# Two transformer layers on one core: attention, the middle and the delta rule's scalars in one block of instructions

## What is computed

```python
x = layernorm(x + attention(x))          # 32 query heads, 8 key heads of 8 dims, rope, causal softmax, @ Wo + bo
x = layernorm(x + ffn8(x))               # silu(x @ w_gate * s) * (x @ w_up * s) @ w_down * s, int8 weights, 1024 wide
x = layernorm(x + delta(x))              # 16 heads of 128
x = layernorm(x + ffn_sign(x))           # relu(x @ sign(up)) @ sign(down)

def delta(x):
    q, k, v = (silu(causal_conv4(x @ W)) for W in (Wq, Wk, Wv))
    alpha, beta = sigmoid(x @ Wa + ba), sigmoid(x @ Wb + bb)
    # per head, for t in order: S = alpha_t * S - beta_t * (S k_t - v_t) k_t^T ;  o_t = S q_t
    return (layernorm(o) * sigmoid(x @ Wg)) @ Wo
```

## Time and profile before

| what | value |
|---|---|
| time of the runs, us | 2126.25, 2126.78 (median), 2129.01 |
| the profiled execution: time, span, us | 2118.2, 2116.5 |
| mean granted TensorE clock, share of full speed | 0.951 |
| busy: PE, DVE, ACT, POOL | 1928.3, 1567.2, 1333.5, 743.7 us |
| attention ends, middle's first product | 511.16, 512.13 us |
| middle ends, delta_heads' first DMA | 667.72, 683.53 us |
| first product of delta_heads | 687.05 us |

### The profile page before, as it was taken

One profiled execution on the slowest core, in us unless ns is written; L12 is line 12 of the kernel. 1 busy time (PEld: TensorE's weight loads), 2 busy tenths in 40 slices (PEclk: granted clock), 3 DMA queues, 4 the chain that ended last, 5 costly groups with the idle time before them and its releaser, 6 DMA issues. The chain is left out here.

```text
span 2116.5 us, 68799 instructions
## 1 busy us (share of the span) xinstructions
PE 1928.3 (91%) x29180; PEld 1458.4 (69%) x29180; DVE 1567.2 (74%) x3017; ACT 1333.5 (63%) x2887; POOL 743.7 (35%) x1037
## 2 busy tenths in 40 slices
PE   7589999996885699999999999999999999999767
PEld 4233333333774578888888888888888888888656
DVE  2699999971754578788888877778788788887356
ACT  1248888884431357677766667667666677676443
POOL 2423444451322223333333333333333333332233
PEclk8779999998996799999999999999999999999879
DMA  3301212101000101011011011011011011010011
GB/s 122 89 21 43 53 31 64 46 18 39 1 1 9 62 12 55 23 42 48 23 49 41 23 44 45 23 37 53 23 35 55 23 40 50 23 34 26 1 43 41
DMA packets 74336, 79.86 MB, mean 38 GB/s; under 512 B 13424, under 2 KB 60912, under 8 KB 74032
## 3 DMA queue, kind: packets, MB, share of 16 engines
q1 hardware_dynamic: 74032, 75.46, 12.3%
HBM read 66.13 MB, written 8.91 MB: 35 GB/s over the span
## 5 line engine op out<-in xcount | busy, mean ns | idle before, releaser
L1711 DVE SCALAR_TENSOR_TENSOR d_acc<-ps,d_par,d_acc 128x1023 f32<-128x1023 f32 (+2 forms) x288 | 365.1, 1268 | 29.5 <-ACT d_acc L1590 28.5
L1403 PE MATMUL ps<-x1p,d_wh 128*128 128x512 f32 x1024 | 358.5, 432 | 16.6 <-DVE d_acc L1711 9.8
L514 ACT ACTIVATE a_prob<-ps 128x512 f32<-128x512 f32 (+2 forms) x640 | 311.3, 560 | 87.3 <-PE ps L483 83.1
L537 DVE TENSOR_REDUCE a_mx<-ps 128x2 f32<-128x1024 f32 (+2 forms) x320 | 336.6, 1111 | 33.5 <-PE ps L467 20.3
L1337 POOL TENSOR_TENSOR d_og_l<-d_o_g,d_og_h 128x512 fp32r<-128x512 f32 x64 | 82.0, 1281 | 426.0 <-ACT d_og_h L1687 426.0
L1403 PE MATMUL ps<-x1p,d_wl 128*128 128x512 f32 x512 | 204.4, 399 | 0.0
L1403 PEld LDWEIGHTS ps<-x1p,d_wh 128*128 128x128 f32 x1024 | 170.8, 194 | 40.1 <-DVE d_acc L1711 10.6
L1590 ACT ACTIVATE d_acc<-ps,d_par 128x512 f32<-128x512 f32 x192 | 149.0, 776 | 72.3 <-PE ps L1403 71.3
L462 PE MATMUL ps<-k,q 48*128 48x512 bf16 (+3 forms) x768 | 142.6, 348 | 34.5 <-DMA k<-scratch_k 20.3
L483 PE MATMUL ps<-q,k 51*128 51x512 bf16 (+2 forms) x640 | 161.4, 364 | 5.6 <-ACT a_prob L514 3.1
L497 PE MATMUL ps<-a_prob,a_v 128*32 128x512 f32 (+3 forms) x1536 | 164.4, 501 | 0.2
(11 more groups left out here) (244 smaller groups left out, 4793.8 us busy)
## 6 DMA issues: line engine op xcount, KB each, us to landing
d_abc<-scratch_alpha SPq DMA_DIRECT2D x32, 512.0 KB, 5.1
d_gb<-scratch_g SPq DMA_DIRECT2D x32, 512.0 KB, 4.0
d_wr<-in_dw SPq DMA_DIRECT2D x16, 512.0 KB, 4.9
scratch_q<-p_parts SPq DMA_DIRECT2D x24, 128.0 KB, 2.4
q<-scratch_q SPq DMA_DIRECT2D x32, 96.0 KB
scratch_y<-a_oT SPq DMA_DIRECT2D x64, 36.0 KB
x_tok<-in_x SPq DMA_DIRECT2D x2, 1024.0 KB
q<-scratch_q SPq DMA_DIRECT2D x32, 64.0 KB
```

The source lines that it names most:

```text
L514: inc(nc.scalar.activation(prob[:, y % PB, g:g + heads, off:], ps[:, PLACE["st", n, x], 0:heads * w].rearrange("p (h c) -> p h c", c=w), A ...
L537: inc(nc.vector.tensor_reduce(out, ps[:, bank:bank + 2, 0:heads * w].rearrange("p r (h c) -> p r h c", c=w), AX.X, ALU.max, negate=True), ...
L1403: last = nc.tensor.matmul(ps[:, bank, :], wp[g][:, k, i, :], x(part), start=(k == 0 and j == 0), stop=(k == KE - 1 and j == 2))
L1711: inc(nc.vector.scalar_tensor_tensor(acc[i][:, d:T], taps[:, 0:T - d], par[p][:, 4 * i + j:4 * i + j + 1], acc[i][:, d:T], ALU.mult, ALU.a ...
```

## The change

The three stages attention, middle and delta_scalars become one block: each function returns its five engine programs, and `one_after_another` writes them behind each other, engine by engine, with semaphores where the barriers were. The phase ends behind delta_scalars.

- **The block around the stages.** Two barriers go. TensorE waits at the end of attention for the last unit's copies out of PSUM. DMAs of the middle (wab, bab, head 0's weights) are issued in load_and_project, behind its own loads. x's transposed copy there takes yT's memory.

```diff
-            load_and_project(nc, ps, x_tok, cst, scratch,
+        load_and_project(nc, ps, x_tok, yT, cst, scratch,
...
+                          "cos": a["c_cos"], "sin": a["c_sin"]}, (w0, ow, hw))
+        with phase(nc) as joint:
+            heads, *rest = attention(nc, layer, ps, x_tok, yT, cst, scratch, ow, w0)
...
+            layers, zs = middle(nc, joint, memory, ps, x_tok, yT, xp, z, cst, ow, w0, hw, *rest)
+            memory.close()
+            one_after_another(nc, joint, heads, layers, delta_scalars(nc, joint, ps, z, sc, cst, alpha_rows, g_rows, zs))
```

```diff
-            E_.walk("POOL", {"v": values, "hide": hide, "cut": cut, "scale": scale})
+        E_.walk("POOL", {"v": values, "hide": hide, "cut": cut, "scale": lambda n: scale(pool, n) if n < UNITS - 1 else None})
...
+        W("nmT", UNITS - 1, 1)
+        W("exp", UNITS - 1, NST)
+        W("o_out", UNITS - 1, 2)
...
+        E_.walk("DVE", {"s1": maxima, "nm": both, "turn": turn, "rec": lambda n: reciprocal(dve, n) if n < UNITS - 1 else None})
+        dve.wait_ge(w.arrived, w.count)
+        for u in range(w.n_up):
+            nc.vector.tensor_copy(w.wu[:, u], w.up[:, u]).then_inc(w.cast, 1)
-            E_.walk("DVE", {"s1": maxima, "nm": both, "turn": turn, "rec": reciprocal})
+    return Programs(sync, gpsimd, tensor, scalar, vector), scaled, reciprocal, scale
...
     self.w, self.n_up = w, w["up"].shape[0]
-        self.arrived, self.count = ctx.enter_context(nc.semaphore("g_w_in")), 16 * (self.n_up + 3)
+        self.arrived, self.count = ctx.enter_context(nc.semaphore("g_w_in")), 16 * (self.n_up + 5)
...
+        self.wu, self.cast = sb("wu", [P, self.n_up, KE, FF], F32R), ctx.enter_context(nc.semaphore("g_cast"))
+        self.wab, self.bab = sb("wab", [P, KE, 2 * H]), sb("bab", [P, 2 * H])
```

```diff
-    with phase(nc) as ctx:
...
-        O_BANK = (6, 4, 2, 6)
+    O_BANK = (6, 4, 6, 6)
+    PROJECT = {1: 2, 5: 3}
...
-        @block.sync
-        def _(sp):
-            sp.dma_start(wab[:], a["wab"].rearrange("(k p) n -> p k n", p=P)).then_inc(ab_in, 16)
-            sp.dma_start(bab[:], a["bab"].partition_broadcast(P)).then_inc(ab_in, 16)
-            hw.fetch(sp, 0)
...
-                if n == 3:
-                    pe.wait_ge(o_freed, 1)
+            pe.wait_ge(scaled, 2 if n < 2 else 4)
+            if n >= 2:
+                pe.wait_ge(o_freed, 2 * n - 3)
...
-                    pe.wait_ge(ab_in, 32)
-                    pe.wait_ge(h_ready, NC * BLK)
+                pe.wait_ge(h_ready, NC * BLK - 1)
...
+        def down_last(c0, c1):
+            if c0 == 0:
+                pe.wait_ge(freed, BLK - 1)
+            for c in range(c0, c1):
+                pe.wait_ge(h_low[c % 2], NC // 2 * (BLK - 1) + c // 2 + 1)
+                for t in range(BT):
+                    for i in range(2):
+                        last = nc.tensor.matmul(ps[:, DOWN + t // 2, (t % 2) * E:(t % 2 + 1) * E], hp[:, 1, i, c, t * P:(t + 1) * P], wd[:, c, :],
+                                                start=(c == 0 and i == 0 and t % 2 == 0), stop=(c == NC - 1 and i == 1), skip_group_check=True)
+            if c1 == NC:
+                last.then_inc(downed, 1)
...
-                    pe.wait_ge(o_freed, 3)
+            if m == 1:
+                pe.wait_ge(o_freed, 2)
...
-            for n in range(3):
+        for n in range(2):
             project(n)
                 up(n, c)
-                    if n == 0 and c == 1:
-                        project(3)
+                if n == 0 and c in PROJECT:
+                    project(PROJECT[c])
...
-            down(BLK - 1, 0)
-            down(BLK - 1, 1)
         logit(0)
-            down(BLK - 1, 2)
-            down(BLK - 1, 3)
+        down_last(0, NC - 2)
         logit(1)
+        down_last(NC - 2, NC)
...
-            for s in range(NU):
-                nc.scalar.activation(wu[:, s], w.up[:, s], ACT.Copy).then_inc(cast, 1)
         nc.scalar.activation(wd[:], w.down, ACT.Copy).then_inc(cast_d, 1)
...
+        hw.halve(nc, pool, 0)
         o_norm.inverse_root(pool, 0)
+        scale(pool, UNITS - 1)
         o_norm.inverse_root(pool, 1)
-            hw.halve(nc, pool, 0)
...
+        pool.wait_ge(g_norm.done, 3)
         low_out(1)
         g_norm.inverse_root(pool, 3)
+        pool.wait_ge(g_norm.done, 4)
...
-            o_close(1)
+        reciprocal(dve, UNITS - 1)
         o_norm.normalise(dve, 0)
-            o_close(2)
+        o_close(1)
...
-                    if m == 3:
-                        o_close(3)
+                if n == 0 and c - 1 in PROJECT:
+                    o_close(PROJECT[c - 1])
...
-            whole_out(2)
         close(3)
         g_norm.statistics(dve, 3, freed)
+        whole_out(2)
         g_norm.normalise(dve, 3)
```

```diff
-    with phase(nc) as ctx:
...
+            if n == 0:
         pe.wait_ge(decays, 1)
...
+        nc.scalar.preload_act_table(ACT.Exp)
         act.wait_ge(mags, 1)
         nc.scalar.activation(em[:], mag[:], ACT.Exp, scale=-1.0).then_inc(exps, 1)
-            nc.scalar.activation(eb[:], z[:], ACT.Exp, scale=-1.0).then_inc(exps, 1)
+        for i in range(2):
+            nc.scalar.activation(eb[:, i], z[:, :, i * H:(i + 1) * H], ACT.Exp, scale=-1.0).then_inc(exps, 1)
+        nc.scalar.preload_act_table(ACT.Ln)
         act.wait_ge(exps, 1)
         nc.scalar.activation(ln1[:], em[:], ACT.Ln, bias=1.0).then_inc(lns, 1)
+        nc.scalar.preload_act_table(ACT.Exp)
...
+        def sigmoid(i):
+            dve.wait_ge(exps, 2 + i)
+            link(nc.vector.tensor_scalar(eb1[:, i], eb[:, i], 1.0, None, ALU.add))
+            link(nc.vector.reciprocal(eb[:, i], eb1[:, i]))
+        dve.wait_ge(zs, 1)
         nc.vector.scalar_tensor_tensor(mag[:], z[:, :, 0:H], -1.0, z[:, :, 0:H], ALU.mult, ALU.max).then_inc(mags, 1)
-            dve.wait_ge(exps, 2)
-            link(nc.vector.tensor_scalar(eb1[:], eb[:], 1.0, None, ALU.add))
-            link(nc.vector.reciprocal(eb[:], eb1[:]))
+        sigmoid(0)
         for b in range(B):
-                nc.vector.tensor_copy(of_units(al[:])[:, b], by_batch(eb[:, :, 0:H])[:, b]).then_inc(al_made, 1)
+            nc.vector.tensor_copy(of_units(al[:])[:, b], by_batch(eb[:, 0])[:, b]).then_inc(al_made, 1)
...
+        sigmoid(1)
+        scu = sc[:].rearrange("p (h b) k c -> p b h k c", b=B)
+        for b in range(B):
+            link(nc.vector.tensor_scalar(scu[:, b, :, S_BETA, :], by_batch(eb[:, 1])[:, b], KK, None, ALU.mult))
```

```diff
-            for dst, name in ((low, "c_low"), (first, "c_first"), (eye, "c_eye"), (ln, "ln")):
-                sp.dma_start(dst[:], a[name]).then_inc(c_in, 16)
...
+            for dst, name in ((low, "c_low"), (first, "c_first"), (eye, "c_eye"), (ln, "ln")):
+                sp.dma_start(dst[:], a[name]).then_inc(c_in, 16)
...
+                if n == 0:
+                    pool.wait_ge(c_in, 64)
+                    nc.gpsimd.tensor_scalar(ln2[:], ln[:], 0.5, None, ALU.mult).then_inc(ln_made, 1)
...
+            nc.gpsimd.memset(dec[:, :, 0:1], 0.0).then_inc(c_made, 1)
+            nc.gpsimd.memset(tn[:], 0.0).then_inc(c_made, 1)
-            nc.gpsimd.memset(tn[:], 0.0).then_inc(c_made, 1)
-            nc.gpsimd.memset(dec[:, :, 0:1], 0.0).then_inc(c_made, 1)
-            pool.wait_ge(c_in, 64)
-            nc.gpsimd.tensor_scalar(ln2[:], ln[:], 0.5, None, ALU.mult).then_inc(c_made, 1)
-            pool.wait_ge(c_made, 9)
+            pool.wait_ge(c_made, 7)
...
+                if n == 0 and h == 0:
+                    pe.wait_ge(bank_made, 1)
...
-            pe.wait_ge(c_made, 9)
...
+                if n == 0:
+                    act.wait_ge(c_made, 7)
...
+                if n == 0 and j == 0:
+                    act.wait_ge(ln_made, 1)
...
-            act.wait_ge(c_made, 9)
...
-            nc.vector.memset(ps[:, INV, :], 0.0).then_inc(c_made, 1)
+            nc.vector.memset(ps[:, INV, :], 0.0).then_inc(bank_made, 1)
...
+                if n == 0:
+                    dve.wait_ge(c_made, 7)
...
-            dve.wait_ge(c_made, 9)
-            dve.wait_ge(c_in, 64)
```

1190 lines of the change are left out of this document (598 added, 592 removed).

## The result

| | kernel before | changed kernel |
|---|---|---|
| time of the runs, us | 2126.25 to 2129.01, median 2127.82 | 2097.07 to 2108.71, median 2103.11 |
| second time (experiment after_again) | 2112.49 to 2138.82, median 2124.00 | 2092.32 to 2104.53, median 2097.81 |
| the first profiled execution: time, span | 2118.2, 2116.5 | 2102.45, 2100.4 |

The changed kernel is faster by 1.1%, clear of the noise: the ratio is 0.9887, with a 95% interval of 0.9861 to 0.9912, and 0.9875 (0.9846 to 0.9905) when it was measured again. The prediction, 2099.2 against 2126.8, is a ratio of 0.9870. But its own sum was made against a profiled execution, and there the gain is 15.8 us (2118.2 to 2102.45) and not 27.6. Where the other 12 went is the question of the experiments.

What follows compares the result with a forecast made beforehand. The prediction took TensorE to bound the heads, leaving serial stops of TensorE around the stage seams to remove; its terms summed to 27.6 us, taken from the median 2126.8 to give 2099.2, range 2090 to 2109.

Steps and rivals of the forecast that it cites:

- Seam, +18.5: Attention to middle: projection 0 starts at ScalarE's last copy, first `up` at 508.7 instead of 527.20, gaining 18.5 us.
- First block, projections -3.6, normalise +1.6, columns -1.2, clock -2.1: Middle's blocks: an extra projection costs 3.6, unstretched normalise saves 1.6, second-block columns cost 1.2, half clock behind seam 2.1 us.
- Casts, -1.7: End of attention: one VectorE weight cast holds up GpSimd's cut of the maxima, costing 1.7 us; ends 0 and 3.4.
- (d): Rival at the end of attention: both casts hold the cut, 1.7 us more, 2100.9; shares the forecast's chance of 0.60.
- End of the middle, +9.0: Last `up` to z: logit 0 fills TensorE's stop, `down_last` and close 3 start sooner, gaining 9.0 us, range 6 to 11.
- Scalars, +3.8, and heads' first product, +3.3: z to heads' first DMA 12.0 us instead of 15.8; then first product after 0.2 us instead of 3.5.
- "The change does nothing there.": Heads: TensorE is busy 1178 of 1200 us at clock 0.99, and their length stays the same.
- (a): Rival at the joined stages: the clock hands gain back, four more half-clock stretches of 2.1 us, 2107.6; chance 0.15.
- (c): Rival at the heads: earlier scalars and first product aren't passed on, 7.1 us gone, 2106.3; chance 0.07.
- (b): Rival: everything fits, no clock dip behind the seam, no cast and cut collision, nothing late, 2093.4; chance 0.13.
- (e): Rival: heads lose clock, so slower; mean 0.968 eats the whole gain, 0.95 gives 2149; chance 0.03.
- (f): Rival: the compiler's order or a wait keeps the stages apart, no gain, about 2126; chance 0.02.

Runs made afterwards that it cites:

- after_again: The changed kernel, unchanged, timed and profiled again: median 2097.81 us, ratio 0.9875 to the kernel before.
- seam_waits: Changed kernel with projection 0 waiting until the last batch is scaled, reciprocal and scale moved ahead of close(0) and the first inverse root: 2115.99 us, ratio 0.9974 to before.
- the pair in step: Changed kernel and kernel before, each with long-fulfilled TensorE waits added (174 and 170 in the middle, 12 per head unit): 2081.00 and 2105.39 us.
- heads_wait_first: Changed kernel with the heads' constants loaded first and waited for by every engine before its first step, as before: 2102.29 us, ratio 0.9906 to before.
- in_step: Changed kernel with only long-fulfilled TensorE waits added, 174 in the middle and 12 per head unit: 2081.00 us, ratio 0.9798 to the kernel before.

## Why the prediction was right, and where not

*Seam, +18.5.* Copy to up fell from 32.09 to 13.40: 18.7, and 19 against the other profiles. The mechanism is the one named; seam_waits shows that it alone makes the gain. The first projection began 0.2 us behind the copy and took 3.83 us until VectorE took it over (3.62 foreseen), and the chain from there to the first `up` 8.8 (9.36). The scale ended 16.3 us behind the copy (16.8 foreseen).

*First block, projections -3.6, normalise +1.6, columns -1.2, clock -2.1: -5.3 together.* Up to up grew by 3.6 to 5.6, on the mean 4.5. The first `up` group's half clock, of which "no row here tells", came in every profile (5.4 to 6.7 us for 16 products, where 3.97 were): 2.4 in the first. Taking the dear end was right. The stretched normalise is gone from the path, and TensorE's wait at the second block grew from 1.10 to 2.03 us, 0.9 where 1.2 was put.

*Casts, -1.7.* This step failed. The lock was weighed rightly, but one cast was taken where both held the cut, so the rival that put both of them there, (d), had the mechanism right. A cast was also taken to be 1.7 us long, after a step of VectorE on f32, and is 1.2. The two errors nearly cancel: the step was held 2.07 us longer (2.35 less 0.28) and TensorE waited 1.7 longer (1.84 and not 0.18), the very number of the forecast. That is luck. The price in time is no constant: 0.5, 1.9, or 6 to 7 us by what the clock does, 7.3 in the first trace. By the Trainium skill's page "SBUF — State Buffer", section "Who interferes with whom", the loser waits out the whole instruction of the other; with one cast the trace agrees, 1.22 us. With two in a row it waited for both.

*End of the middle, +9.0.* 6.9 in the first profile, 8.2 to 8.5 in those where TensorE's clock held better, 8 to 9 undone. In the first, `down_last` took 8.65 us for 48 products and not 7.0, partly at half clock, and close 3 began 6.6 us sooner; with 7.3 us for the 48 it began the 8.0 us sooner that were foreseen. What is missing in both is behind it. The last turn (1.95) and the last logit (3.62) were at half clock, in every profile of the changed kernel, where they were taken to be warm: 0.3 us gained from close 3 to z and not 1.0. Both steps rested on the clock and were set too well; the range of 6 to 11 held. (The sum took 48 `down` products at the mean rate of both old groups, but the last 16 at the faster one's, 2.0 and not 2.35; they took 2.15.)

*Scalars, +3.8, and heads' first product, +3.3.* z to product fell by 6.2 and not 7.1: 3.05 of it is the constants, 2.4 the order of the scalars, and what is left, 0.8, is put down to the barrier, for which 1.3 was taken; no run takes the barrier alone. z's end to the next stage's first DMA is 12.6 and not 12.0: VectorE's chain is 11.2 of it (11.0 foreseen), and the step to the next stage 1.4, for which the 0.97 of the other seam was taken. The first product stands 0.5 behind that DMA and not 0.2.

*"The change does nothing there."* For the heads that held in the pair in step (1252.6 and 1253.0), but not as a statement on the profiled executions, whose ways differed by over 10 us. The step that failed is the first sentence of the sum: one profile's gain was carried over to the median unchanged. The first pair of profiles differs by 16.1 us in span (the terms are rounded): +4.6 ahead of attention's last unit (a clock of 0.83 from 20 to 60 us before, 1.00 after), -7.3 casts, +18.7 seam, -3.7 first block on, +6.9 end, +6.2 scalars and first product, -9.2 behind it. Of these the first, most of the last and most of the second belong to the execution and not to the change, as far as the second profiles and the pair in step show. The others give 28.1, and with 0.5 to 1.9 for the cast 26 to 27.6. The times gave 24.0, 26.5 and, in step, 25.5. So by the medians 27.6 was right to 1 to 4 us. The intervals reach from 19 to 33 us of gain, so that closeness is in part luck, and where the rest is can't be said from these runs.

*Rivals.* (a), the clock hands it back, had 2107.6, a ratio of 0.9910; it is outside the second interval and just inside the first. By the rows the clock did take part in three terms, but not as four more stretches of 2.1: the first `up` group was in the sum, the end of the middle fell 0.8 to 2.1 short, and the cut cost 0.5 to 7. (c), the heads don't pass it on, is out by the pair in step, where unit 3 still starts 4.8 and 6.9 us nearer to z, and heads_wait_first points the same way; (b), everything fits, is out by the half clock in the first `up` groups and by the held cut; (e) is out by a clock of 1.00 from 800 to 1900 us in both kernels; (f) by the seam.

Both signs that the prediction named as those of being wrong came up in the first profile. The heads' stretch was not of the same length, and of the 12.5 us up to unit 31 the stops of over 0.4 us make 7.5. And the first `up` groups ran at 0.50 from 511.27 to about 516.5, some 5 us, where the work behind the old seam did for some 4.

## What to carry to other kernels

Price a serial seam by its chain and ask what of the next stage needs nothing of it: that alone was worth 19 us here. Do not read a difference of a few us between two single profiles as the doing of an edit before the same kernel was profiled twice, and look for idle time that the profile gives to no engine. Where TensorE has long rows of very small products, an edit anywhere ahead of them, even of an instruction that does nothing, can move the time: 84 waits made 2% here. Compare at equal places of the marks, or hold a loop's instructions near a multiple of 256 and put the marks into long products, as in_step does.

## What the runs showed that I had not expected

- TensorE stops where the count of its instructions passes a fixed place modulo 256: all 135 stops of over 0.4 us in the 11 profiles that had them lie at 192 to 196. They cost 9 to 20 us here (1101.5 against 1110.9 to 1121.4 from unit 3 to 31), 40 with the marks put among the small products, nothing with them in long ones. The instruction queue's packets grow with the count, 233 for 59,653 and 235 for 60,211, and every one of the stops ends 1.20 to 1.65 us behind the end of its packet.
- A long-fulfilled wait in TensorE's program costs nothing behind a 512-column product; 558 of them, by where they moved the marks, made the kernel 16 to 19 us faster (0.9798 against 0.9875 and 0.9887).
- Two VectorE casts from int8 to fp32r in a row (1.2 us each) hold a GpSimd step of 0.28 us for both: 2.35 us.
